# A fused decoder layer on one core: the loop over the cross-attention heads written out on TensorE, VectorE and ScalarE

## The reference, cut to what matters

```python
qh = _split_heads(jnp.einsum('bnq,qi->bni', x, Wq))          # 8 heads of 128
kh = _split_heads(jnp.einsum('bmc,ci->bmi', context, Wk))    # heads x (b*m = 4096 keys) x 128
vh = _split_heads(jnp.einsum('bmc,ci->bmi', context, Wv))
sim = jnp.einsum('hid,hjd->hij', qh, kh) * SCALE
mean = jnp.mean(sim, axis=-1, keepdims=True)
sim = (sim - mean) * 1.5 + mean
attn = jax.nn.softmax(sim, axis=-1)
out = jnp.einsum('hij,hjd->hid', attn, vh)
out = out.reshape(HEADS, b, n, DIM_HEAD).transpose(1, 2, 0, 3).reshape(b, n, HEADS * DIM_HEAD)
return jnp.einsum('bni,iq->bnq', out, Wout) + bout
```

## Time and profile before

| | before |
|---|---|
| median of three runs | 2859.33 us |
| the profiled execution's own time | 2863.82 us |
| its span | 2862.0 us |
| TensorE matmul busy | 2619.1 us (92%) |
| TensorE weight load busy | 2340.1 us (82%) |
| VectorE busy | 1970.0 us (69%) |
| ScalarE busy | 1603.2 us (56%) |
| GpSimd busy | 132.6 us (5%) |
| mean granted TensorE clock | 0.962 of full speed |

### The profile page before, as it was taken

How to read it: one execution, slowest core, us unless ns; L and a number is a source line. 1 busy time by engine, 2 the same in 40 slices (tenths; PEclk the granted TensorE clock), 3 DMA queues, 4 the chain that set the end, 5 groups by cost and what they waited for, 6 DMA issues and landing times. The chain is left out here.

```text
span 2862.0 us, 50044 instructions
## 1 busy us (share of the span) xinstructions
PE 2619.1 (92%) x17664; PEld 2340.1 (82%) x17664; DVE 1970.0 (69%) x3680; ACT 1603.2 (56%) x3011; POOL 132.6 (5%) x153
## 2 busy tenths in 40 slices
PE   6477777899999998999899989998999999999976
PEld 4466666599879987998799879987998899889975
DVE  6366668577667766776677667766776677677776
ACT  4366662366646664656465646655565556556644
POOL 0450003000000000000000000000000000000003
PEclk9699998799999999999999999999999999999997
DMA  5563322400110011001100110012001100110000
GB/s 178 161 167 80 76 52 70 175 16 22 53 67 23 15 60 61 23 15 60 62 22 15 60 68 16 15 60 68 16 15 60 68 16 15 60 62 22 9 12 30
DMA packets 94930, 153.36 MB, mean 54 GB/s; under 512 B 48400, under 2 KB 62096, under 8 KB 93680
## 3 DMA queue, kind: packets, MB, share of 16 engines
q1 hardware_dynamic: 90176, 137.48, 15.2%
q0 software_dynamic: 3200, 12.59, 1.3%
q10 hardware_dynamic: 1328, 0.39, 0.1%
HBM read 123.02 MB, written 23.20 MB: 51 GB/s over the span
## 5 line engine op out<-in xcount | busy, mean ns | idle before, releaser
L1293 ACT CAST pt_hi<-xt_ps 128x512 fp32r<-128x512 f32 x1024 | 591.7, 585 | 578.3 <-PE xt_ps L1263 560.8
L1359 DVE TENSOR_TENSOR pt_lo<-xt_ps,pt_hi 128x512 fp32r<-128x512 f32 x1024 | 705.2, 689 | 275.4 <-ACT pt_hi L1293 271.9
L1348 DVE TENSOR_SCALAR_CACHE_REDUCE xprobs<-xs_ps 128x1024 f32<-128x1024 f32 x512 | 626.7, 1224 | 188.5 <-PE xs_ps L1212 183.4
L1274 PE MATMUL xo_ps<-pt_hi,v_hi 128*128 128x256 f32 x2048 | 649.5, 317 | 1.3 <-DVE pt_lo L1359 1.3
L1299 ACT ACTIVATE xprobs<-xprobs,xneg_max 128x1024 f32<-128x1024 f32 x512 | 591.4, 1155 | 23.6 <-DVE xneg_max L1354 23.6
L1263 PE MATMUL xt_ps<-ident,xprobs 128*128 128x128 f32 x4096 | 604.1, 272 | 0.0
L1274 PE MATMUL xo_ps<-pt_lo,v_hi 128*128 128x256 f32 x2048 | 577.6, 282 | 0.0
L1274 PE MATMUL xo_ps<-pt_hi,v_lo 128*128 128x256 f32 x2048 | 576.0, 281 | 0.0
L1263 PEld LDWEIGHTS xt_ps<-ident,xprobs 128*128 128x128 f32 x4096 | 485.1, 140 | 60.7 <-issue 6.9
L1274 PEld LDWEIGHTS xo_ps<-pt_hi,v_hi 128*128 128x128 f32 x2048 | 388.8, 190 | 4.0 <-DVE pt_lo L1359 1.3
L1274 PEld LDWEIGHTS xo_ps<-pt_lo,v_hi 128*128 128x128 f32 x2048 | 389.4, 190 | 1.9
(11 more groups left out here) (203 smaller groups left out, 2864.7 us busy)
## 6 DMA issues: line engine op xcount, KB each, us to landing
blocks<-ctx_split SPq DMA_DIRECT2D x68, 768.0 KB, 5.8
xq<-x_split SPq DMA_DIRECT2D x64, 512.0 KB, 3.3
q_st<-rel_split SPq DMA_DIRECT2D x64, 128.0 KB, 2.6
q_st<-q_split SPq DMA_DIRECT2D x192, 32.0 KB, 2.1
k_st<-k_split SPq DMA_DIRECT2D x192, 32.0 KB, 1.9
ctx_split<-ctx_out POOLq DMA_DIRECT2D x8, 768.0 KB, 4.2
v_st<-v_split SPq DMA_DIRECT2D x64, 64.0 KB, 2.3
x_split<-xq_out SPq DMA_DIRECT2D x8, 512.0 KB, 4.8
```

The lines of the kernel that those rows point to most:

```text
L1274: last = pe.matmul(o_ps[:, 0:GQ], v[:, vs], pt[:, c % 3, GQ * j:GQ * (j + 1)], start=c == 0 and j == 0 and m == 0, stop=c == PIECES - 1 an ...
L1293: act.copy(pt_hi[:, c % 3, :], t_ps[:, c % 3, :]).then_inc(t_rounded, 1)
L1348: dve.tensor_scalar(probs[:, par if kind == "A" else 1 - par, t, CHUNK * i:CHUNK * (i + 1)], s_ps[:, buf, :], LOGIT, None, ALU.mult, ALU.m ...
L1359: dve.tensor_tensor(pt_lo[:, c % 3, :], t_ps[:, c % 3, :], pt_hi[:, c % 3, :].bitcast(F32), ALU.subtract).then_inc(t_ready, 1)
```

## The change

`run_heads` loses its outer hardware loop. The eight heads are now called one after another with `h` a constant of the program. The inner loop at L1034 stays a hardware loop in each of the eight copies; SyncE's program is not touched. No item, no list and no order changes.

```diff
             step(STEP_8, G, STEP_AT[G])
             step(AFTER, G + 1, AFTER_AT)
 
-    with eng.Fori(0, XH - 1) as h:
-        head(h, False)
-    head(XH - 1, True)
+    for h in range(XH):
+        head(h, h == XH - 1)
```

## The result

The kernel with the eight heads written out takes 2821.11 us (median of four runs, 2814.59 to 2821.53), against 2859.36 us before (four runs, 2859.01 to 2864.02). The ratio is 0.9851, with a 95% interval of 0.9839 to 0.9863: 1.5% faster. The prediction said 2818 us, with a range of 2811 to 2828. The profiled execution took 2821.53 us, 42.3 less than that of before.

The account below looks back on a forecast made before the run. TensorE was taken to bound each head, so only its stalls and slow clock could be won. Six turns gave 43.4 us, other terms nothing: 2863.8 to 2820.4 or 2859.3 to 2815.9 us, with 2818 taken between; range 2811 to 2828.

Parts of the forecast that it names:

- Six turns become fall-throughs: Outer head loop, L1048 branch to L1034 MOVE: six turns fall from 54.6 to 47.4 us each, a gain of 43.4 us.
- The cross-check: At the six turns: 36.3 us less TensorE idling plus 7.1 us of slow clock on value matmuls make 43.4 us.
- The other engines' turns add nothing: VectorE's and ScalarE's turn stalls (23.9 and 19.1 us) go too, but lie beside TensorE's longer one: no gain.
- ScalarE's table load: 1.28 us behind each turn, inside 3 us for which ScalarE waits for VectorE: adds nothing if it goes.
- Register instructions at nothing: Wait counts outside the inner loop become constants: nothing taken, at most 1.9 us for the range.
- What is late next: Context blocks, asked for 6 us sooner after each turn, still land 2.6 us early: nothing taken, 1 us a head for the range.
- More code to fetch at nothing: Eight copies of a head instead of one looped: straight code is fetched while it runs, so no cost.
- The inner loops keep their place: The jump back at L1034 stays cheap in all eight copies (longest branch seen 247 ns); forecast chance 0.80.
- The rivals that lost one or all of the inner jumps: L1034 jumps turn dear, 7.2 us each: some lost, 2825 to 2840 us, chance 0.08; all lost, 2874 us, slower 0.03.
- The median: Run median 4.5 us below the profiled execution: new median 2820.4 us if that lies in the turns, 2815.9 if elsewhere.

Follow-up runs that it names:

- pe_only: Kernel before with the eight heads written out on TensorE alone, VectorE and ScalarE still looping over seven: 2861.52 us, ratio 0.9998.
- two_turns: Kernel before with TensorE, VectorE and ScalarE looping over pairs of heads in three passes, last two heads written out: 2834.09 us, ratio 0.9905.
- inner_too: Changed kernel with the inner loop written out as well on TensorE, VectorE and ScalarE: 2819.69 us, ratio 0.9839 to the kernel before.
- all_engines: Changed kernel with the inner loop and SyncE's two loops written out too, no loop left in the stage: 2823.18 us, ratio 0.9856 to the kernel before.
- after_again: The changed kernel, unaltered, measured once more beside later experiments: 2820.53 us, ratio 0.9846 to the kernel before.
- pe_act: Kernel before with heads written out on TensorE and ScalarE, VectorE still looped: 2856.27 us, ratio 0.9981.

## Why the prediction was right

- **Six turns become fall-throughs, 43.4 us.** Right to the tenth in the profiled execution: 1969.8 became 1926.4 us. The sum had rested on the one turn that the trace of before shows untaken, and all seven written-out heads behave as that one did, with a period of 275.2 us. The cross-check beside it, 36.3 us of idling and 7.1 of slow clock, met the same 43.4 by luck. Between the MOVEs TensorE is busy for 11.5 us less and idle for 31.9 less. The 7.1 left out the score matmuls, which ran slowly too (the first three pairs take 2.72 us after the turn and 1.49 at the fall-through the earlier trace rows), and the 36.3 left out that TensorE, once it restarts early, waits for VectorE's `v_lo` again: in front of L1195 for 5.9 us in all before, and 10.3 after. The two errors cancel.
- **The other engines' turns add nothing.** Right for this change, which takes all of them away together, and misleading beyond it. I had called TensorE's turn the longest and the others covered by it. The runs show that TensorE's turn and VectorE's hide each other: with either one left, a turn still costs 6.4 to 6.9 us. What I had missed is VectorE's second stall, 2.15 us in `pe_only`, which in the trace of before lies inside a wait for TensorE. My expectation for `pe_only`, 3.3 to 5 us a turn, failed on that: it counted one stall, of 4.1 us.
- **ScalarE's table load** went, and cost nothing while the others stood too. With ScalarE alone looped a turn costs 1.0 us.
- **Register instructions at nothing.** Right: `two_turns` keeps them in six heads and pays only for its turns, and `inner_too`, which has none left, is as long as the changed kernel to 0.1 us.
- **What is late next.** Nothing: behind the places where the loop turned no wait for `blocks` appears. The one in the stage (1.1 us in front of L1179) lies at its very start, before head 0, and the kernel before has it too. With SyncE's loops gone as well (`all_engines`) nothing changes.
- **More code to fetch at nothing.** Right, and one remark was too careful. I allowed some dozens of instruction packets more; there are fewer. Probably each taken outer jump had thrown away packets that were fetched ahead; no run shows that by itself. The changed kernel's queues, which had 128 and 98 packets before:

```profile
q8 instruction: 114, 1.87, 0.3%
...
q14 instruction: 63, 0.52, 0.1%
```

- **The inner loops keep their place.** Right, with room to spare: TensorE's body could grow from 942 to 1542 instructions and VectorE's from 143 to 243 before a jump was missed. The rivals that lost one or all of the inner jumps were farther off than the 0.11 that I gave them.
- **The median.** I had left open whether the 4.5 us between the profiled execution of before and the median lay in the turns. Both have a part. The single turns of the kernel before differ (the period is 281.5 to 283.5 us), and more scatter comes from ahead of the stage: the first MOVE comes at 598.0 us in the changed kernel and at 591.1 in `after_again`, while the way to the last MOVE is 1926.4 and 1926.3 us. The 42.3 us between the two profiled executions are the 43.4, less 1.5 by which the first MOVE came later, plus 0.4 that the rest behind the last MOVE got shorter. The medians fell by 38.3 us only, from 2859.36 to 2821.11; where the kernel before ran beside the experiments its medians were 2861.9 to 2863.7, and `after_again` is 43.2 us below. So the 43.4 are right for the stage, and 2818, the middle of two guesses about the scatter, was 3 us low. Why the earlier stages differ by 7 us between executions stays open.

## What to carry to other kernels

In this kernel a hardware loop is free while its body is short and dear once the jump goes back too far: a branch of 0.2 us up to 1542 instructions on TensorE, 3.3 to 3.4 us from 1742 on, and 6 to 8 us where bulk loads run beside it. Count turns, write out the long outer loop and leave the short inner one; and do it on every engine whose turn lies at the same place, since with either TensorE or VectorE left looped almost nothing was gained. Where the last pass is already written out in the same kernel, as here, the way into it shows what the others will gain before anything is built. A cross-check whose parts add up to the same number proves little as long as each part has left something out.

## What the runs showed of the hardware that was not expected

- An instruction fetch is held up by data: the same outer jump takes 6.2 to 7.9 us beside 3 MB of block loads and 3.3 to 3.9 us without them, and the whole difference lies ahead of the start of the instruction packet.
- A second fetch can follow the first: in `pe_only` VectorE stood for 3.89 us, ran one instruction and stood for 2.15 us more, and in `pe_act` each of its two stalls (4.09 and 2.45 us) has its own instruction packet.
- TensorE's missed jump shows as a long branch instruction (3.3 to 3.4 us), VectorE's and ScalarE's as a short one (0.04 to 0.07 us) with the stall behind it; looking for long branches alone misses two engines of three.
